# Fillers on TensorE in the threshold search and ahead of the gate's largest product, with other tiles and another order of maxima for GpSimd's integer products

## The reference

```python
x = x + xattn0(layernorm(x), ctx_1024, W, b)      # two linear maps and a bias
x = x + ffn0(layernorm(x), Wg, W1, W2, W3)        # 8 experts, each takes its 512 best rows
x = x + xattn1(layernorm(x), ctx_1024, mask, W_out)   # 16 heads, 154 keys
x = x + ffn1(layernorm(x), w_gate, w_up, w_down)  # quantized, inner width 768
```

```python
# ffn0: the choice of rows
scores = (x_flat @ Wg.T).T
top_vals, token_idx = jax.lax.top_k(scores, capacity)      # capacity = 512 of 4096 rows for each expert
# ffn1
act_qdq(x) = clip(round(x / s), -32768, 32767) * s,  s = max|x| / 32767 over the whole tensor
up = act_qdq(x @ dequant(w_up).T);  gate = act_qdq(x @ dequant(w_gate).T)
sig = fixed_qdq_u16(sigmoid(gate))
gate = act_qdq(gate * sig);  o = act_qdq(gate * up)
return o @ dequant(w_down).T
```

## Time and profile before

| | |
|---|---|
| median of 3 runs | 755.82 us (755.79 to 755.91) |
| the profiled execution | 754.42 us, its span 752.6 us |
| TensorE busy | 641.6 us, 85% |
| VectorE busy | 621.7 us, 83% |
| ScalarE busy | 529.7 us, 70% |
| GpSimd busy | 305.9 us, 41% |
| mean granted TensorE clock | 0.938 |

### The profile page before, as it was taken

The page is one execution under the profiler, slowest core; times in us unless marked ns, Lnnn a source line. Parts: engine busy times, 40 slices in busy tenths (PEclk is TensorE's granted clock), DMA queues, the critical chain, the costliest instruction groups (busy, mean ns, idle before and its releaser), DMA issues.

```text
span 752.6 us, 12183 instructions
## 1 busy us (share of the span) xinstructions
PE 641.6 (85%) x4268; PEld 386.0 (51%) x4268; DVE 621.7 (83%) x1304; ACT 529.7 (70%) x713; POOL 305.9 (41%) x249
## 2 busy tenths in 40 slices
PE   6883049999999789999999999989999995029998
PEld 5762025666666544456455645644444443006887
DVE  5898897989898699886888877988997998995433
ACT  2134664776774649898998986666657996996873
POOL 5345616577774436451343110015412443892000
PEclk9997559999999999999999999999999998559999
DMA  9946665567753580000040001021103412101443
GB/s 311 331 135 208 212 168 161 123 159 187 188 110 38 100 268 1 2 22 1 1 155 30 2 29 45 13 84 57 57 0 119 162 70 98 56 0 57 153 129 112
DMA packets 59542, 78.17 MB, mean 104 GB/s; under 512 B 7904, under 2 KB 48224, under 8 KB 59488
## 3 DMA queue, kind: packets, MB, share of 16 engines
q1 hardware_dynamic: 49936, 60.58, 24.3%
q0 software_dynamic: 7872, 14.82, 9.0%
q10 hardware_dynamic: 1680, 2.08, 0.8%
HBM read 50.07 MB, written 27.39 MB: 103 GB/s over the span
## 4 chain that ended last, share of the span: by engine, by line
PE 58%; DVE 17%; ACT 10%; POOL 2%; issue 2%; DMA 1%; DVEq 0%; POOLq 0%; ACTq 0%
PE bank L2586 11%; PE bank L2319 8%; PE bank L2260 8%; PE bank L2618 5%; PE bank L1597 4%; PE bank L1654 4%; PE bank L1639 3%; PE bank L1707 3%; DVE above L852 2%; PE bank L1669 2%; DVE qx L1320 2%; PE bank L1612 2%; PE bank L1678 2%; PE bank L1634 2%; ACT wgateT L2209 1%
## 5 line engine op out<-in xcount | busy, mean ns | idle before, releaser
L1320 DVE TENSOR_REDUCE qx<-bank 128x4 f16<-128x616 f32 x128 | 98.0, 801 | 21.7 <-PE bank L1597 20.2
L1453 ACT ACTIVATE x<-bank,bic 128x512 f32<-128x512 f32 x160 | 104.6, 690 | 15.9 <-PE bank L1639 12.1
L2260 PE MATMUL bank<-ux,uwh 128*128 128x512 f16 x384 | 91.2, 380 | 0.4 <-ACT ux L2154 0.3
L2260 PEld LDWEIGHTS bank<-ux,uwh 128*128 128x128 f16 x384 | 37.4, 98 | 45.9 <-issue 0.8
L1597 PE MATMUL bank<-Kb,qTb 128*128 128x308 bf16 x256 | 52.6, 297 | 2.0 <-DVE qx L1320 1.1
L2260 PE MATMUL bank<-ux,uwl 128*128 128x512 f16 x192 | 49.3, 379 | 0.0
L1245 POOL CAST qx<-q 128x1024 f16<-128x1024 f32 x8 | 8.5, 1066 | 98.0 <-PE bank L1612 87.3
L1639 PE MATMUL bank<-qT,K 128*128 128x512 f16 x128 | 44.4, 380 | 0.3
L2319 PE MATMUL bank<-uwh,oh 128*128 128x256 f16 x192 | 43.4, 273 | 0.3 <-ACT oh L2232 0.2
L2267 PE MATMUL bank<-uwh 128*128 128x512 f16 x46 | 12.5, 424 | 36.4 <-DVE peak L1990 36.4
L2539 ACT ACTIVATE wgateT<-bank,qs 128x512 f32<-128x512 f32 x32 | 21.9, 686 | 30.5 <-PE bank L2586 30.3
(11 more groups left out here) (464 smaller groups left out, 1887.1 us busy)
## 6 DMA issues: line engine op xcount, KB each, us to landing
x_dram<-x SPq DMA_DIRECT2D x4, 1024.0 KB, 5.3
xr<-in_w1T SPq DMA_DIRECT2D x8, 512.0 KB, 4.0
xr<-in_w3T SPq DMA_DIRECT2D x8, 512.0 KB, 4.9
xr<-in_w2T SPq DMA_DIRECT2D x8, 512.0 KB, 6.7
row_dram<-xn SPq DMA_DIRECT2D x8, 512.0 KB, 3.2
x_dram<-xr SPq DMA_DIRECT2D x8, 512.0 KB, 2.9
x<-x_dram SPq DMA_DIRECT2D x8, 512.0 KB, 4.6
xT<-in_xT SPq DMA_DIRECT2D x7, 512.0 KB, 6.6
```

The costliest lines, as they stand in the source:

```text
L1320: dve.tensor_reduce(qx[:, k, g * GH:(g + 1) * GH, MROW].rearrange("p (u h) -> p u h", u=2), pair[i][:].rearrange("p (u x) -> p u x", u=2)[ ...
L1453: act.activation(dst, S_[u % 2], ACT.Exp, bias=bic[:, s // 2, int(tail):int(tail) + 1], scale=1.0 / 16).then_inc(p_done, 1)
L2260: mm = pe.matmul(bank[j][:, m * TB:(m + 1) * TB], w[:, c * HI + cols:c * HI + cols + P], x[:, part, c * TB:(c + 1) * TB], start=(w is uwh ...
```

## The change

Three things are done at once; no arithmetic of the result is altered.

1. In the search and the lists, 5 fillers go ahead of the first count, 6 into each of the 10 digits (3 right behind the sums of the digit before, 2 once VectorE's first count of the digit is made, 1 once its second is), 5 behind the transposes of `ex`, 2 ahead of the sum of the weights' squares, and 6, 4, 4, 1, 3 and 1 around the transposes of `slot` and the first two lists. A filler here is a product of the 128 x 128 identity in f32 with itself, written to a part of PSUM that nobody reads then.
2. Ahead of spread 2 the 16 fillers in one go become 8, 6 and 5, which wait until 21, 22 and 23 of the 24 products with their maxima are made.
3. In the integer stage GpSimd still takes 11 tiles, now 4, 5, 7, 8, 12, 13, 16, 17, 19, 20 and 23, of which ScalarE makes the up integers of 16, 19 and 23. VectorE takes the maximum of its tiles 0 and 1 right behind their products, that of its other tiles one place later, and that of GpSimd's tiles two places later.

```diff
+                def filled(n, at):
+                    for _ in range(n):
+                        pe.matmul(at, ident, ident, start=True, stop=True)
+
+                searching, listing = bank[3][:, 512:512 + P], bank[1][:, 0:P]
+                filled(5, searching)
                 pe.wait_ge(d_cnt, 1)
                 pe.matmul(bank[1][:, 0:1], blk16[:], cnt0[:], start=True, stop=True).then_inc(d_pe, 1)
                 for n in range(DIGITS + 1):
                     levels = LEVELS if n < DIGITS else 1
+                    if n < DIGITS:
+                        filled(3, searching)
+                        pe.wait_ge(d_cnt, LEVELS * n + 2)
+                        filled(2, searching)
+                        pe.wait_ge(d_cnt, LEVELS * n + 3)
+                        filled(1, searching)
                     pe.wait_ge(d_cnt, LEVELS * n + levels + 1)
...
                 halves(bank[2], ex)
+                filled(5, searching)
                 pe.wait_ge(d_mid, 4)
...
+                filled(2, searching)
                 pe.wait_ge(d_place, 1)
                 pe.wait_ge(e_wh, 1)
                 pe.matmul(squares, ones16[:], sums16[:, 0:2], start=True, stop=True).then_inc(e_sum, 1)
+                filled(6, listing)
                 pe.wait_ge(d_mid, 5)
                 halves(bank[0], slot)
+                filled(4, listing)
+                pe.wait_ge(d_hot, 1)
+                filled(4, listing)
+                pe.wait_ge(d_hot, 2)
+                filled(1, listing)
...
                 listed(0)
+                filled(3, listing)
+                pe.wait_ge(d_hot, 5)
+                filled(1, listing)
                 listed(1).then_inc(d_sum, 1)
...
-            POOL_AT = tuple(range(3, FT, 2))
+            POOL_AT = (4, 5, 7, 8, 12, 13, 16, 17, 19, 20, 23)
             DVE_AT = tuple(i for i in range(FT) if i not in POOL_AT)
-            UP_BY_ACT = POOL_AT[2::3]
+            UP_BY_ACT = (16, 19, 23)
...
-                for i in range(FT):
+                def due(i):
+                    return i + 2 if i in POOL_AT else i + (i >= 2)
+
+                for i in range(FT + 2):
...
-                    if i:
-                        largest_out(i - 1)
-                largest_out(FT - 1)
+                    for k in sorted(range(FT), key=lambda k: k in POOL_AT):
+                        if due(k) == i:
+                            largest_out(k)
...
-                for _ in range(16):
-                    pe.matmul(bank[3][:, 0:P], ident, ident, start=True, stop=True)
+                for left, n in ((3, 8), (2, 6), (1, 5)):
+                    pe.wait_ge(k_p, FT - left)
+                    for _ in range(n):
+                        pe.matmul(bank[3][:, 0:P], ident, ident, start=True, stop=True)
                 spread(2, 2)
```

## The result

| | median (range, runs) | against the kernel before beside it |
|---|---|---|
| before | 756.16 us (755.40 to 756.82, 12) | |
| after | 757.62 us (755.02 to 759.91, 12) | 1.0019, 95% interval 1.0010 to 1.0028 |

The changed kernel is 1.46 us or 0.19% slower: within the 0.2% that I called no difference, and clearly not zero. Its runs also spread more, with a standard deviation of 1.40 us against 0.46 (0.74 to 1.34 in the other sets of runs of the kernel before). The profiled execution took 756.37 us with a span of 754.6 us, 1.95 us above that of before.

A forecast was written before the change was run, and what follows sets the result against it. TensorE, with 58% of the chain of waits, was taken to bound the kernel, VectorE's chain in two half-clock stretches. Terms +1.15, -0.2 and -0.2 us on 754.42, plus 1.4 for the runs, gave 756.6 us, range 753.7 to 758.8.

The forecast's parts named there:

- Start: Ahead of the search's first count: five fillers at half clock delay the first sum by 1.7 us, at full clock 0.65.
- Digits: Search digits: fillers fit at full clock and cost nothing; faster sums give -0.35 us, between 0 and -1.0.
- Lists: List 1's 16 products at full clock remove VectorE's 0.2 us wait: -0.2 us.
- TensorE with fillers it already had, whose clock is full from 113.6 us anyway: Behind the lists: TensorE's existing fillers are late next, already at full clock; no cost was entered.
- Spread 2: Transposes and broadcast of spread 2 may run at full clock: -0.2 us, between 0 and -0.4.
- Integer stage: VectorE ends 1.0 us earlier without waiting for GpSimd, but 21 fillers hold spread 3's transposes, leaving 0.2 us.
- Rival 3: Start costs 1.7 to 2.2 us and nothing is given back: 757.5 to 758.3 us; chance 0.2.
- Rival 2: Clock stays at half through the search, so fillers lengthen each digit by 0.3 us: 761.1 us; chance 0.1.
- rival 1: Start costs only 0.6 us, digits, lists, spread 2 and integer stage give all they can: 753.8 us; chance 0.2.

The follow-up runs named there:

- All mended: Changed kernel with 2 fillers ahead of the first count, 5 and 8 wide ones ahead of lists 2 and 3, 5, 5, 5 ahead of spread 3: 756.00 us, 1.0000.
- The trimmed version: Kernel before with parts 2 and 3, but 5, 5, 5 fillers instead of 8, 5, 8 ahead of spread 3: 754.56 us, ratio 0.9982; repeated, 0.9974.
- part 1 alone: Kernel before with only the change's fillers in the search and the lists: 759.05 us, ratio 1.0035.
- the start alone: Kernel before with only the five fillers ahead of the first count: 758.24 us, ratio 1.0031.
- the lists added: The trimmed version plus the lists' fillers, with 5 and 8 wide fillers ahead of lists 2 and 3: 759.15 us, ratio 0.9998.

## Why the prediction was right, and where it was not

The forecast was 756.6 us in 753.7 to 758.8 and "within 0.2%" at 0.5; it is 757.6 us and +0.19%. The number is near, and that is partly luck: in the profiled execution the start cost 1.05 us less than I took, and a step that I had put at nothing cost 1.74.

- **Start, +1.7 us: the mechanism holds, the size is that of one of two clock levels.** I took the half clock since it had fallen at 65.8 us in the one trace that I had. Waits of 1.64, 1.73 and 1.73 us at half clock and 0.60 at full bear out both ends of the step. The failing is that I read one execution's clock as fixed. The two prices go with the wider spread of the runs, which comes and goes with the five fillers.
- **Digits, -0.35 us: not seen.** From line 838 to 914 the six traces with the digits' fillers take 34.47 to 35.77 us, 35.41 in the mean, and the eight without 34.54 to 35.50, 35.02 in the mean. A sum takes 178 ns at full clock (11 of line 1034, 177 to 178) against 186, and the digits with no other influence last 2.56 us in both kernels: line 857 starts at 75.12, 77.68 and 80.24 before and at 75.85, 78.41 and 80.96 after. VectorE still waits 0.21 to 0.23 us there. The Trainium skill's formula (TensorE: Matmul & The Clock Gate, Single matmul latency) has, as an estimate for 4 columns, 18 ns a sum; the trace shows 8, so the formula is too high, though nearer than my 0.05 us a digit. The -0.18 us in the table above is within what the stretch varies by itself: 34.65, 34.84, 34.96, 35.08, 35.21 and 35.50 us in six kernels whose search is the same code. In the last of these some of VectorE's small steps are longer where GpSimd's pass over `xn` (line 1003) lies beside them (line 891 at 0.37 and 0.44 us against 0.15); whether this is the cause wasn't tried.
- **Lists, -0.2 us: right** (-0.28: 12.37 or 12.38 us from `hi` to the last ids in the traces with the fillers, 12.65 to 12.83 without).
- **"TensorE with fillers it already had, whose clock is full from 113.6 us anyway": this is the step that failed**, a term that I had put at nothing and that is the largest, +1.74 us in the profiled execution. I had taken the full clock for a property of the place, and TensorE's fillers for what comes last there. A TensorE that had run fast and then idled for the marks lost the clock at 115.1. With the gaps open it was lost between 111.0 and 117.5 us in four traces of four, with the gaps filled in none of three. Of the 1.74 us, 0.78 are the clock's alone; for the other 0.96 the rows that landed late would have been enough. All mended shows that price by itself, with the clock full: 6.98 us against 5.68.
- **Spread 2, -0.2 us between 0 and -0.4: right in its ends**, -0.41 where the clock held, 0 in the trace where it didn't. The Trainium skill (same page, Part 4: PE-mode transpose) says that the full clock doesn't take effect for transposes. For these f32 ones the traces disagree once more, 0.38 against 0.58 us.
- **Integer stage: right.** VectorE 0.91 us earlier (forecast 1.0), no wait for GpSimd, 0.17 us left (forecast 0.2), since 21 fillers stand ahead of the transposes. The trimmed version shows the reason: 0.78 us more came out by removing six fillers.
- **Rivals.** Rival 3 (start costs, little comes back, 757.5 to 758.3 us) gives the median best, but for a reason that it doesn't name, since in the trace parts 2 and 3 gave back 0.58 us. Rival 2 shows in single digits only. Of rival 1 the condition "if the fillers before spread 3 don't hold it" was made true by hand, and parts 2 and 3 then gave 1.5 and 2.3 us by the medians.

## What to carry to other kernels

A filler ahead of a critical instruction in an engine's queue is a cost at the worst clock, not at the one in your trace: give it only as many as fit at half speed, and count again the fillers that stand behind the stretch you speed up. When a chain on one engine is shortened, look at once for padding on the engine that takes over; taking out six fillers paid here, and adding fillers to the search did not. Tiles and order of an in-order queue are one choice: each half alone made this stage longer (1.28 and 0.26 us), both together shorter (0.91). And before a late instruction is put down to the clock, look whether what it reads had landed.

## What the runs showed of the hardware

- The granted clock fell beside the same, unchanged work anywhere between 62.0 and 68.0 us, by execution and chip, in thirteen traces of fourteen, and not at all there in the changed kernel. One trace of before gives one sample of it.
- A filler of two f32 products of 128 columns: 0.22 us apart at full clock, 0.43 at half (ten instructions in 1.35 and 2.39 us). A bf16 sum of 4 columns on its own gains 8 ns of 186 from the doubled clock, a spread's pair of f32 transposes 0.20 of 0.58 us.
- Work with f32 fillers between waits brought the clock back and held it through ten digits, but in all five other traces with the digits' fillers it fell once more between 96 and 103 us, around those of `ex` and `slot`, and not in the profiled changed kernel. What tells these apart wasn't found.
- A gathered part of 128 rows mostly landed 2.8 to 3.9 us behind its issue, but in five traces one of the first four took 4.1 to 5.1 us (the changed kernel, part 1 alone, all mended, the start alone, the lists added). In each of the five a 16 KB packet of a queue that loads instructions ran beside it. In the changed kernel it is seen between 114 and 117 us:

```profile
q8 instruction: 1, 0.02, 1.8%
```

  Three other traces had such a packet near and 3.5 to 3.8 us, so it isn't shown to be the cause; nor was it tried whether the fillers' own instructions bring it there.
